# A language-model tower on one core: the token ids of the first two sequences spread by TensorE instead of through DRAM, and a rearranged setup

## The reference

```python
# embedding: position, bracket nesting depth and segment, through one matrix
opens  = (t == 40) | (t == 123) | (t == 91)
closes = (t == 41) | (t == 125) | (t == 93)
s = cumsum(opens - closes, axis=1)
nesting  = clip(s - minimum(cummin(s), 0), 0, 15)
segments = cumsum(t > 39990, axis=1) % 8
h = concatenate([pos_table[pos], nest_table[nesting], seg_table[segments]]) @ W
# linear attention with 8 heads of 64, chunks of 128 tokens
h = h + attention(layernorm(h)) @ w_out.T + b_out
# mixture of 8 experts, two per token
h = h + experts(layernorm(h), top 2 of softmax gates)
```

## Time and profile before

| | us |
|---|---|
| median of 3 runs | 421.6 (420.7, 421.6, 424.39) |
| profiled execution, from first to last instruction | 438.2 |
| PE busy in it | 363.8 (83%) |
| DVE busy | 313.1 (71%) |
| ACT busy | 253.5 (58%) |
| POOL busy | 244.2 (56%) |

### The profile page before, as it was taken

One profiled execution on the slowest core, in us unless ns is written; L12 is line 12 of the kernel. 1 busy time (PEld: TensorE's weight loads), 2 busy tenths in 40 slices (PEclk: granted clock), 3 DMA queues, 4 the chain that ended last, 5 costly groups with the idle time before them and its releaser, 6 DMA issues.

```text
span 438.2 us, 12358 instructions
## 1 busy us (share of the span) xinstructions
PE 363.8 (83%) x3127; PEld 321.2 (73%) x3127; DVE 313.1 (71%) x1170; ACT 253.5 (58%) x705; POOL 244.2 (56%) x566
## 2 busy tenths in 40 slices
PE   1679999999999999999996435999999999999300
PEld 1457888787787877878885313999999999999300
DVE  7666878788777887777974561777777777678154
ACT  1246677776667676676754101777777777677200
POOL 6111117776667767677677660466666665766500
PEclk9989999999999999999999556999999999999855
DMA  5355500001000000000000031222222222221198
GB/s 136 92 158 159 155 1 21 21 15 31 27 27 13 13 27 27 27 20 13 20 28 28 28 101 48 61 74 73 77 71 76 70 75 70 70 76 58 54 308 243
DMA packets 39227, 29.54 MB, mean 67 GB/s; under 512 B 4679, under 2 KB 35778, under 8 KB 39202
## 3 DMA queue, kind: packets, MB, share of 16 engines
q1 hardware_dynamic: 27858, 16.30, 13.6%
q0 software_dynamic: 4352, 9.45, 6.0%
q10 hardware_dynamic: 6992, 3.50, 2.8%
HBM read 16.50 MB, written 12.73 MB: 67 GB/s over the span
## 4 chain that ended last, share of the span: by engine, by line
PE 63%; DVE 14%; DMA 8%; issue 6%; SPq 5%; DVEq 1%; POOL 1%; ACT 1%; another core or an unknown queue 0%; POOLq 0%; ACTq 0%
PE ps_out L1320 7%; PE ps_oy L1332 7%; PE ps_vc L1332 7%; PE ps_q L1320 6%; PE ps_k L1175 5%; PE ps_out L1213 4%; DMA row_of<-ids_dram 4%; PE ps_oy L1228 4%; PE ps_vc L1175 3%; SPq L480 3%; PE ps_oy L1221 3%; PE ps_q L1175 3%; PE ps_vc L1203 3%; PE ps_ln L1312 2%; PE ps_k L1320 2%
## 5 line engine op out<-in xcount | busy, mean ns | idle before, releaser
L607 POOL DMA_INDIRECT y_dram<-heads_out,place x72 | 73.8, 1025 | 29.9 <-issue 25.9
L578 POOL DMA_INDIRECT slots_dram<-rows,row_id x64 | 63.3, 988 | 19.5 <-issue 19.5
L734 ACT ACTIVATE k_prime<-ps_q,b_T 128x128 f32<-128x128 f32 x108 | 31.8, 365 | 19.8 <-PE ps_q L1320 19.8
L734 ACT ACTIVATE k_prime<-ps_out,b_T 128x128 f32<-128x128 f32 x108 | 31.8, 366 | 19.0 <-PE ps_out L1320 18.9
L544 POOL TENSOR_TENSOR rstd<-moments,ln_eps 128x2 f32<-128x2 f32 x32 | 6.2, 195 | 62.3 <-DVE moments L821 62.1
L1332 PE MATMUL ps_oy<-w_tile,k_prime 128*128 128x128 f32 x288 | 38.1, 275 | 0.4 <-issue 0.4
L1332 PE MATMUL ps_vc<-w_tile,k_prime 128*128 128x128 f32 x288 | 38.1, 275 | 0.1
L1320 PE MATMUL ps_out<-sT,w_tile 128*128 128x128 f32 x288 | 38.1, 275 | 0.0
L539 POOL TENSOR_TENSOR spare<-minus_half,ln_eps 128x2 f32<-128x2 f32 x89 | 18.1, 204 | 35.1 <-ACT heads_out L743 22.1
L1213 PE MATMUL ps_out<-context,qT 128*128 128x130 f32 x256 | 36.1, 283 | 1.5 <-issue 0.8
L1091 DVE COPY w_tile<-w_all 128x640 f32 x72 | 36.0, 499 | 1.5
(11 more groups left out here) (232 smaller groups left out, 1028.2 us busy)
## 6 DMA issues: line engine op xcount, KB each, us to landing
qkv_rows<-slots_dram SPq DMA_DIRECT2D x72, 72.0 KB
w_all<-in_L_ffn_W SPq DMA_DIRECT2D x1, 2048.0 KB, 13.5
w_all<-in_L_ffn_W SPq DMA_DIRECT2D x8, 256.0 KB, 4.6
y_first<-y_dram SPq DMA_DIRECT2D x8, 256.0 KB, 5.6
y_second<-y_dram SPq DMA_DIRECT2D x8, 256.0 KB, 6.0
out<-y_first ACTq DMA_DIRECT2D x8, 256.0 KB, 5.5
y_dram<-heads_out,place POOLq DMA_INDIRECT x72
slots_dram<-rows,row_id POOLq DMA_INDIRECT x64
```

The source lines that it names most:

```text
L578: nc.gpsimd.indirect_dma_start(slots_dram[:, :], bass.IndirectOffsetOnAxis(row_id[:, place_of(p, a), j, k:k + 1], 0), rows[:, place_of(p, ...
L607: nc.gpsimd.indirect_dma_start(y_dram[:, :], bass.IndirectOffsetOnAxis(place[:, a, :], 0), y[:, a, :], None).then_inc(s_placed[a], 16)
L734: last = nc.scalar.activation(hT[:, a % 2, c, :], ps_up[a % 2][0][:, c * P:c * P + P], ACT.Relu, bias=b1_T[:, bass.ds(experts[0] * FC + c, ...
```

## The change

What it does, strand by strand (line numbers of the new kernel where they differ):

- Ids: PE copies the rows of sequences 0 and 1 over the partitions. POOL makes a small 0/1 matrix `seq_rows` (16 x 2 x 2 x 96), and four products of it with `nesting` and `segments` write the two rows to the PSUM tile `ps_q` (L1148, L1149); `hot(0)` and `hot(1)` read them there, one right after the other. The way through DRAM stays for the others, in two groups: sequences 2 and 3 (`s_row_next`), then 4 to 15 (`s_row`).
- Bracket sum: one running value `fall` with three opening and three closing codes in turn, the sign turned once (five two-input instructions after the first), a running maximum instead of a minimum.
- Table: split in place, the bias part first and by itself, each later part on fewer partitions; the position part is copied by ACT instead of DVE.
- Transfers: the small tables ahead of `tok_rows` on SP, and ahead of `out_rows` on ACT; `out_rows` is last of the attention weights.
- PE: the small table's products and the position products come right after the first transposes, then the ids, then all of the attention weights, with the transposes of `out_rows` last.
- Constants: `pad_rows` and `empty_rows` are filled by POOL in step `p == 1` of the attention stage (`make_padding`), with a semaphore of their own.
- The products without a reader read `nesting` (16 partitions, 256 columns) and there are 16, 24 and 4 of them instead of 9, 12 and 2.

```diff
@@ SP
-            sp.dma_start(tok_rows[:, :, :], tok_w.rearrange("(a p) h -> p a h", p=P)).then_inc(s_emb_w, 16)
             sp.dma_start(pos_rows[:, :, :], pos_table[0:S, :].rearrange("(a p) h -> p a h", p=P)).then_inc(s_emb_w, 16)
-
             sp.wait_ge(s_zero, 1)
             load_tables(sp, 0)
             load_tables(sp, 1)
+            sp.dma_start(tok_rows[:, :, :], tok_w.rearrange("(a p) h -> p a h", p=P)).then_inc(s_emb_w, 16)
+            sp.wait_ge(s_zero, 3)
...
-            for first, last, done in ((0, HEAD_SEQS, s_row_head), (HEAD_SEQS, B, s_row)):
+            for first, last, done in ((HEAD_SEQS, NEXT_SEQS, s_row_next), (NEXT_SEQS, B, s_row)):
@@ POOL
+            step.done(nc.gpsimd.memset(seq_rows[:, :, :, :], 0.0))
...
+            nc.gpsimd.affine_select(out=seq_rows[:, :, :, :], in_=seq_rows[:, :, :, :], compare_op=ALU.is_equal, fill=0.0,
+                                    base=0, pattern=[[0, 2], [-1, HEAD_SEQS], [0, TR]], channel_multiplier=1)\
+                .then_inc(s_seq_rows, 1)
...
+                if isinstance(p, int) and p == 1:
+                    make_padding()
@@ ACT
-            act.dma_start(out_rows[:, :], w_out[:, :]).then_inc(s_att_w, 16)
             act.wait_ge(s_zero, 1)
             load_tables(act, 2)
+            act.wait_ge(s_zero, 2)
             for r in range(2):
                 act.dma_start(proj_diag[DH * r:DH * r + DH, DH * r:DH * r + DH], proj[:, :]).then_inc(s_att_w, 16)
+            act.dma_start(out_rows[:, :], w_out[:, :]).then_inc(s_att_w, 16)
...
+            act.wait_ge(s_wT, 1)
+            nc.scalar.activation(pos_part[:, :, :], ps_ln[:, 0:2 * D], ACT.Copy).then_inc(s_pos, 1)
@@ DVE
-            step.done(nc.vector.tensor_scalar(delta[:, :], tokens[:, :], 40, None, ALU.is_equal))
-            for code in (123, 91):
...
-            step.done(nc.vector.tensor_scalar(other[:, :], tokens[:, :], 41, None, ALU.is_equal))
-            for code in (125, 93):
...
-            step.done(nc.vector.tensor_tensor(delta[:, :], delta[:, :], other[:, :], ALU.subtract))
+            step.done(nc.vector.tensor_scalar(fall[:, :], tokens[:, :], 40, None, ALU.is_equal))
+            for code, op in ((123, ALU.add), (91, ALU.add), (41, ALU.subtract), (125, ALU.add), (93, ALU.add)):
+                step.done(nc.vector.scalar_tensor_tensor(fall[:, :], tokens[:, :], code, fall[:, :], ALU.is_equal, op))
...
+            def split_table(n, whole):
+
+                step.done(nc.vector.tensor_copy(table[:, n, :], whole))
+                step.done(nc.vector.tensor_tensor(rest_one[:, n, :], whole[0:2 * SLOT], table[0:2 * SLOT, n, :], ALU.subtract))
+                step.done(nc.vector.tensor_copy(table[0:2 * SLOT, n, :], rest_one[:, n, :]))
+                step.done(nc.vector.tensor_tensor(rest_two[:, n, :], rest_one[0:SLOT, n, :], table[0:SLOT, n, :],
+                                                  ALU.subtract))
+                return nc.vector.tensor_copy(table[0:SLOT, n, :], rest_two[:, n, :])
...
             def hot(p, a):
-                wait(dve, s_emb, p - 1)
-                nc.vector.tensor_scalar(one_hot[:, a, :], row_of[:, span(p * S, S)], table_id[:, 0:1], None,
-                                        ALU.is_equal).then_inc(s_hot, 1)
+                if isinstance(p, int) and p < HEAD_SEQS:
+                    ids = ps_q[0:TR, p * S:p * S + S]
+                else:
+                    wait(dve, s_emb, p - 1)
+                    ids = row_of[:, span(p * S, S)]
+                nc.vector.tensor_scalar(one_hot[:, a, :], ids, table_id[:, 0:1], None, ALU.is_equal).then_inc(s_hot, 1)
@@ PE
+            pe.wait_ge(s_ids, 2)
+            pe.wait_ge(s_seq_rows, 1)
+            for b in range(HEAD_SEQS):
+                nc.tensor.matmul(ps_q[0:TR, b * S:b * S + S], seq_rows[:, 0, b, :], nesting[:, :], start=True, stop=False)
+                last = nc.tensor.matmul(ps_q[0:TR, b * S:b * S + S], seq_rows[:, 1, b, :], segments[:, :],
+                                        start=False, stop=True)
+            last.then_inc(s_heads, 1)
```

More of the change, by code:

```diff
@@ L493, in _ @@
                                     pattern=[[-1, P]], channel_multiplier=1).then_inc(s_ident, 1)
+            step.done(nc.gpsimd.memset(seq_rows[:, :, :, :], 0.0))
+            for k in range(2):
+                step.done(nc.gpsimd.memset(seq_rows[:, k, :, :].rearrange("p b (r c) -> p b r c", r=PARTS)
+                                           [:, :, :, k * SLOT // 2:k * SLOT // 2 + SLOT // 2], 1.0))
+            nc.gpsimd.affine_select(out=seq_rows[:, :, :, :], in_=seq_rows[:, :, :, :], compare_op=ALU.is_equal, fill=0.0,
+                                    base=0, pattern=[[0, 2], [-1, HEAD_SEQS], [0, TR]], channel_multiplier=1)\
+                .then_inc(s_seq_rows, 1)
             nc.gpsimd.memset(minus_half[:, :], -0.5)
@@ L627, in _ @@
             act.wait_ge(s_t1, 3)
-            nc.scalar.activation(out_w[:, :, :], ps_qT[:, :], ACT.Copy).then_inc(s_hi, 1)
-            act.wait_ge(s_t1, 4)
             nc.scalar.activation(qkv_hi[:, 2, :], ps_vc[:, :], ACT.Copy).then_inc(s_hi, 1)
@@ L634, in _ @@
             nc.scalar.activation(qkv_hi[:, 1, :], ps_out[:, 1, :], ACT.Copy).then_inc(s_hi, 1)
+            act.wait_ge(s_t1, 4)
+            nc.scalar.activation(out_w[:, :, :], ps_qT[:, :], ACT.Copy).then_inc(s_hi, 1)
             def xT_high(p, a):
@@ L791, in _ @@
-            step.done(nc.vector.tensor_tensor(rest_two[:, :, :], rest_one[:, :, :], split_mid[:, :, :], ALU.subtract))
-            step.done(nc.vector.tensor_copy(split_lo[:, :, :], rest_two[:, :, :]))
-            for r, part in enumerate((split_hi, split_mid, split_lo)):
-                last = nc.vector.tensor_copy(table[SLOT * r:SLOT * r + SLOT, :, :], part[SLOT * r:SLOT * r + SLOT, :, :])
-            last.then_inc(s_wTc, 1)
+            def split_table(n, whole):
[5 more added lines that the diff above has]
+                return nc.vector.tensor_copy(table[0:SLOT, n, :], rest_two[:, n, :])
@@ L946, in even @@
                 if isinstance(p, int) and p + 2 == HEAD_SEQS:
+                    dve.wait_ge(s_row_next, 16 * PARTS)
+                if isinstance(p, int) and p + 2 == NEXT_SEQS:
                     dve.wait_ge(s_row, 16 * PARTS)
-                if live(p + 2):
+                if isinstance(p, int) and p == -2:
+                    for q in range(HEAD_SEQS):
+                        hot(q, q)
+                elif live(p + 2) and not (isinstance(p, int) and p + 2 < HEAD_SEQS):
                     hot(p + 2, a)
@@ L1143, in _ @@
                 last.then_inc(s_wT, 1)
+            for c in range(HC):
+                last = nc.tensor.transpose(ps_qT[:, c * P:c * P + P], out_rows[:, c * P:c * P + P], idn)
+            last.then_inc(s_t1, 1)
             pe.wait_ge(s_wTc, 1)
+            pe.wait_ge(s_pos, 1)
             pe.wait_ge(s_const, 1)
@@ L1150, in warm_up @@
                 for _ in range(count):
-                    nc.tensor.matmul(ps, part_ones[:, :], row_of[:, 0:HD], start=True, stop=True)
+                    nc.tensor.matmul(ps, part_ones[0:B, :], nesting[:, :], start=True, stop=True)
             def embed(p, a):
```

96 lines of the change are left out of this document (44 added, 52 removed).

## The result

The changed kernel takes 425.25 us (median of 16 runs, 424.51 to 426.44), the kernel before 423.28 us (419.98 to 425.57) on the same chip: a ratio of 1.0054, with a 95% interval of 1.0033 to 1.0074. The forecast was 418.4, with a range of 416.0 to 421.4.

The account below looks back on a forecast made before the run. PE is nearly full in steady state, so only setup before the first `embed` and the third `one_hot`'s wait count: 438.2 - 2.15 - 1.05 = 435.0 profiled, carried over as 421.6 - 3.2 = 418.4 us, range 416.0 to 421.4.

Parts of the forecast that it names:

- PE's start: Setup: PE's first work moves from 9.12 to 8.3 us, as small tables no longer queue behind `out_rows` (0.81 us).
- The first embed at 15.8: End of setup on PE: first `embed` at 15.8 instead of 17.94, gain 2.15 us, bounds 0.15 and 1.35.
- If the level rises again 4.6 us after the start (12.9): Setup: PE's clock reaches its upper level at 12.9, so the sixteen steps of L1161 take 2.1 us.
- Rival 3: Slower: PE stays at the lower clock level in setup and first q, k, v products; +1.9 us, 423.5; chance 0.07.
- DVE until then: Setup on DVE: `nesting` ends at 10.2, two `one_hot` at 14.0, the first 2.2 us ahead of PE.
- port rule: Setup: POOL and VectorE block each other in two-port mode or with two SBUF inputs; the second doubted, up to 0.97 us.
- 16 x 256 = 4096 columns without a reader: Behind first `embed`: 4096 columns fit as the 4608 did (2.10 us); the later 24 and 4 equal 12 and 2.
- The third one_hot: Attention stage: DVE's 1.68 us wait for ids goes; PE gains 1.05 us, bounds 0 and 1.68.
- The padding on POOL: POOL's 2.5 us of padding behind 53.94 delays `shift` 0.1 us inside ACT's idle time: zero, bound +0.2.
- If the time moves in the expert stage: One of the signs listed as showing the prediction wrong: a change of time in the expert stage.

Follow-up runs that it names:

- the new trace of before: Profile of the kernel before, run once more unchanged on the first chip: 423.52 us, ratio 1.002, span 420.4 us.

## Why the prediction was wrong

By its own steps:

- **PE's start**, 9.12 to 8.3: measured 8.09. Right. Over all traces it is 8.97 to 9.15 in the four of the old setup and 8.09 to 8.36 in the ten of the new, 0.85 us earlier on average, where 0.81 was expected.
- **The first embed at 15.8, a gain of 2.15**: wrong. It stands at 17.75, a gain of 0.2, hardly above the lower bound of 0.15. The step that failed is "If the level rises again 4.6 us after the start (12.9)". The sixteen steps of L1161 took 3.62 us, not 2.1. Rival 3 named this course (its chance was 0.07) and priced its setup part rightly. In a second trace of the kernel after, the sixteen took 2.81 and `embed` stood at 17.14; in the eight other traces that keep or nearly keep the new order they took 3.57 to 3.73. In three more traces of the old order of the setup (1.95 to 2.19) they ran at the upper level, all or all but the first few. Estimated from the spacing of the steps, the level rose 3.0 to 4.8 us after PE's first work in the four traces of the old order, and 7.5 to 10.5 us after it in the ten of the new: the 4.6 us, read from one trace, was a property of the old order. Nor is the gain of 0.2 a firm one: without the weights moved behind it, `embed` stands at 17.14 to 18.14 in seven traces of the new order and at 17.04 to 17.98 in four of the old. What in the new order holds the level down, its pauses, the four products of the ids on 16 partitions ahead of the weights, or the moved transposes, wasn't tried.
- **DVE until then**: `nesting` was expected at 10.2 and ended at 9.49, the two `one_hot` at 14.0 and ended at 14.02, ahead of PE. Right. L770's 1.93 us is gone (it stood beside both of POOL's padding memsets, 6.41 to 8.46, and not only beside L528), and the five of L782 took 0.44 each though POOL's L516 (0.97 us) ran beside them. In the trace of the kernel before with 16 partitions the two of L772 took 0.43 each beside L528 (1.05 us). So the half of the Trainium skill's port rule that the prediction doubted, for two inputs in SBUF (GPSIMD Engine Reference, Specifications), doesn't show here either.
- **"The 16 x 256 = 4096 columns without a reader fit in it as the 4608 did ...; their 24 and 4 later equal 12 and 2"**: wrong, and the step that set the sign. Columns and time were indeed equal (5.30 us against 5.19), but that isn't what these products are for. No row stood behind the claim that they act alike, and none was looked for in the expert stage. The price is 3.5 to 3.8 us by the medians; in the pair of traces it is 3.7 from the first slot transpose on and 0.6 behind the setup's 16. The sum had it at nothing.
- **The third one_hot, 1.05**: right for the trace that it was read from. From the start of v's products to the product behind `heads_out` that trace has 2.18 us (35.12 to 37.30) and the kernel after 1.10: 1.1 won. Against the new trace of before, with its longer wait, it is 1.7 (2.79 us there). But the kernel before with 16 partitions has 1.10 too, without any of the change, as its DVE missed POOL's padding. So this gain is one that some executions of the kernel before have already, and what it is worth in the median isn't shown.
- **The padding on POOL, nothing**: right. ACT's `rows` at 57.15 waited for nothing.

The sum by its measured terms, the new trace of before against the trace after: -0.2 up to the transpose of x, +0.6 in q's first products, -1.7 at the third `one_hot`, -0.1 up to the first slot tile, +3.7 from there: +2.3 us, which is the difference of the two spans. Rival 3 had the mechanism, PE at its lower level, and put most of it in the wrong place: in the setup and the first q, k and v products rather than in the expert stage behind the products without a reader. That its total of +1.9 us lies next to the measured 2.0 is luck. "If the time moves in the expert stage" stood among the signs of being wrong, and it did.

## What to carry to other kernels

Work whose result nobody reads is there for what it does to the chip, so an edit to it must be priced by that, with the rows right behind it, and not by its columns or its time. Keep such products on many partitions (16 and 96 are what was tried here), and put them just ahead of the work they serve: with 40 of them the level was up, and after 2.41 us of idle time it was gone. And where an order puts work that isn't wanted yet in front of the chain's first step, moving it behind that step can be worth more than the edit under study (0.6 to 0.9% here).

## What was unexpected of the hardware

- Products on 16 partitions take as long as products on 96 (5.30 us for 24 at the lower level, 1.92 against 1.91 for 16 at the upper) and didn't bring PE's clock to its upper level: 0.50 to 0.51 in the windows from 246 to 260 us, against 0.95 (before, 252 to 260) and 0.79 (after with 96). The Trainium skill (TensorE: Matmul & The Clock Gate, The HAM clock gate) ties the level to how busy the engine was lately; the rows of busy time don't tell these two kernels apart (before, 7.49 us of idle time, 5.19 of products, 0.89 of idle time; after, 7.49, 5.30 and 0.86), so that by itself doesn't foretell which of them comes up. Products on 96 partitions don't always raise the level in time either: in the second trace of the kernel with the weights behind, 24 of them took 5.30 us, all at the lower level, and of all traces only the new one of before has its first group of six at the upper level (0.90 us, where the others have 1.48 to 1.51).
- The data play no part in it that shows: zeros on 96 partitions did what numbers did (0.9962 and 0.9965), and numbers on 16 partitions still cost (1.0036).
- One and the same program ran at 422.6 us on one chip and at 448.5 and 448.64 on two others. Single instructions are equally long (q's product 0.48 us in both, the clock at 1.00 from 80 to 220 us). What differs is idle time in the attention loop: in the kernel before on the first chip PE was busy for 79.96 of 80 us from 80 to 160, in the one with the padding moved on the second for 72.36. From 90 to 210 us VectorE's `h` waited for `embed` 1.1 us a time in the one with the padding moved (8.7 us in 8) and 0.27 in the other (2.4 in 9). The trace shown ahead of the prediction, with its 438.2 us, is of the idle kind in part (76.26 of 80 us), so the gaps that the prediction read in it aren't those of most runs. The cause stays open.
